# Attention in a macaron block: late features, turns and projections of group 5, and the placing of the first half moved to other steps

## The chip, the cores and the metric

One core of a Trainium2 chip runs the whole program. The metric is the device time of one execution in microseconds. The kernel before was timed in three runs; their median is 1233.25 us.

## What is computed

The reference takes x of 2 x 2048 tokens of 256 features and adds three blocks to it, each on a layer-normalized x: half of a mixture-of-experts feed-forward (16 experts in 4 groups of 4, top 2 of the best 2 groups, and a shared expert), an attention, and the same feed-forward again.

```python
x = x + 0.5 * ffn(layernorm(x), ...)
x = x + attn(layernorm(x), ...)
x = x + 0.5 * ffn(layernorm(x), ...)
```

The attention has 16 heads. Per head, the query and the key are each the normalized exterior product (6 numbers) of two projections to 4 numbers; scores are their product with a fixed signed permutation, times 6 to the power −0.5, causal, with a softmax over 2048 keys; values have 16 numbers per head; the result is projected by W_o and added to x.

## The kernel before

The program is one long sequence for each engine, ordered by semaphores. First comes the first feed-forward, then a stage called `lines`, then the attention (`attend`), then the second feed-forward by halves of the tokens (`ffn_by_halves`), whose routing for the first half of the tokens is done during the attention.

**`lines`** (L1258 to L1651) goes over 8 blocks of 512 tokens and makes from each the queries' and keys' features (fp16, split in a high and a low part) and the values. PE transposes the features ("turns", L1420), ScalarE evicts them from PSUM (L1496) and SP stores them to DRAM. The last block's features are done late, inside the first group of the attention: `copy_last` (two ScalarE copies, L1468 and L1469, after DVE's subtractions up to L1646), four `turn_last` parts on PE (L1449, two for queries and two for keys) and four `keep_last` evictions on ScalarE (L1461). SP stores queries and keys of that block after the second and the fourth eviction.

**`attend`** (L1686) goes over 8 groups g = 0 to 7: batch 0 has groups 0 to 3, batch 1 has groups 4 to 7 (`GATE` is 4), each with 4 heads. A group has four query chunks of 512 (`qc` 0 to 3) against key tiles of 128. The scores of the 40 units (one query chunk, one key tile, four heads) are packed in N = 48 strips of three PSUM banks, and each strip is one step i = 0 to 47:

- PE: `scores(g, i)` (L1877) into one of two strips of PSUM, then the value matmuls of the units that are due (`weigh`, L1903, four heads of 32 columns side by side), then what else is assigned to the step: a use of a spare bank, a late turn, a half projection (`project`, L1917).
- ScalarE: one exponential over the strip (L2017), from PSUM to a ring of 8 strips in SBUF. Scores of step i wait for the exponential of step i − 2.
- POOL: the causal masks (`cut`, L2027): ten selects for each chunk's diagonal, in its four strips (0 to 3, 8 to 11, 20 to 23 and 40 to 43): two, two, three and three.
- DVE: for each chunk, after its last values: copy of the sums (L2072), shuffle, reciprocal and product (L2075 to L2083), the "division"; then the additions of projections to x (`add_half`, L2097), statistics for the second normalization (L152) and pieces of routing.

Which values are due at which step is computed (L1727 to L1734). Values are due at steps 4, 6 to 9, 12, 14 to 17, 19 to 21, 24, 26 to 29, 31 to 33, 35 to 37, 39 to 41, 44 and 46 to 49 (48 and 49 are the next group's 0 and 1). Steps 6, 14, 26 and 46 have two narrow units (384 and 256 columns), steps 7, 15, 27 and 47 one of 128 and one of 512, the others one of 512. So steps 5, 10, 11, 13, 18, 22, 23, 25, 30, 34, 38, 42, 43 and 45 have no value matmuls ("free" steps). Chunk 0 and 2 sum in bank 6, chunk 1 and 3 in bank 7.

What else is done at a step is written by hand in tables (L1742 to L1763): the half projections of even groups at 22 and 25, of odd groups at 22, 25, 34, 38, 42 and 45; in group 5 ("shared") the last four are at 39, 41, 43 and 45. Projections use bank 7 for chunk 0 and 3 and bank 6 otherwise. In group 4 and 5 the normalized tokens of the first half are turned (`turn_at`, PE L1191) and copied by DVE (`keep_tiles`, L2110); the routing's logits are made at (5, 34) (PE L1959) and turned at (5, 38) (L1965); the pairs are counted at (6, 45) (PE L1196 and L1197). `rested` counts uses of the spare banks, so that each waits for the one before. DVE does the softmax, the choice and the weights in group 6, the placing (`routing.place`, L1109 to L1145) in group 7 after chunk 0, and `name_experts` after chunk 1. `add_among_marks` (L2165) holds the rest: the marks of rows (L1152), tiles (L1158) and tokens (L1163, L1167) among the additions of chunks 1 and 2 of group 7; PE's `invert` needs them after the attention.

An order by hand is one per engine: an instruction that waits holds all that stand behind it on its engine.

## Time and profile before

| | us |
|---|---|
| runs of the kernel before | 1233.25, 1230.09, 1234.88 (median 1233.25) |
| the profiled execution | 1235.22 |
| its span (first to last instruction) | 1233.5 |
| attention in it, first exponential to last values | 403.8 to 913.6 |
| PE busy | 1046.1 (85%) |
| ACT busy | 873.3 (71%) |
| DVE busy | 772.3 (63%) |
| POOL busy | 457.8 (37%) |

Times in the rows are microseconds from the span's start. PE is TensorE (matmuls), ACT ScalarE, DVE VectorE, POOL GpSimd, SP SyncE. A row of a timeline has the start, the length, the engine, the line of the kernel, the operation with its output and input, the shape and how many equal ones were merged; what stands in brackets is the idle time of the engine just before and what released it. A row of windows has the stretch and its length, then busy time and, in parentheses, instructions of PE, PE's weight loads, DVE, ACT and POOL, then TensorE's granted clock (1.00 is 2.4 GHz, 0.50 is 1.2 GHz), the DMA's busy share and GB/s.

### The profile page before, as it was taken

What the parts mean: (1) busy time and instruction counts of PE and PEld (TensorE: products, weight loads), DVE (VectorE), ACT (ScalarE), POOL (GpSimd) and SP (SyncE); (2) the same over time, 40 slices, a digit from 0 to 9 for tenths busy, and PEclk for the clock granted to TensorE, in tenths of its full rate; (3) what the DMA queues carried; (4) which work ended last, traced back from release to release, by engine and by line L of the source; (5) the groups of instructions that cost most, each with busy time, mean ns of one, the idle gap of its engine ahead of it and who ended that gap; (6) DMA issues with size and microseconds to landing.
All of it is one profiled execution on the core that took longest, in us unless ns stands there. A gap on an engine that the chain in (4) does not pass through costs nothing.

```text
span 1233.5 us, 23530 instructions
## 1 busy us (share of the span) xinstructions
PE 1046.1 (85%) x7487; PEld 570.4 (46%) x7487; DVE 772.3 (63%) x1565; ACT 873.3 (71%) x1250; POOL 457.8 (37%) x675
## 2 busy tenths in 40 slices
PE   3998999877887688988898989897999886967894
PEld 3457888744555212222222222221245685957752
DVE  6897777665997423444355565675786873645845
ACT  4246776624878999999999999999972463745610
POOL 1004555375630324331313234313133446564363
PEclk8999999998989799999999999999999997998997
DMA  8902544443756211010101130201009443443453
GB/s 294 279 4 78 161 152 156 130 127 108 219 176 213 88 31 52 18 52 18 52 18 53 35 104 19 74 15 52 2 31 318 127 137 124 155 137 114 131 167 120
DMA packets 125717, 133.79 MB, mean 108 GB/s; under 512 B 13224, under 2 KB 111888, under 8 KB 125616
## 3 DMA queue, kind: packets, MB, share of 16 engines
q1 hardware_dynamic: 109056, 90.95, 23.2%
q0 software_dynamic: 14448, 39.47, 11.1%
q10 hardware_dynamic: 2112, 2.10, 0.5%
q8 instruction: 55, 0.90, 0.3%
q14 instruction: 46, 0.38, 0.1%
HBM read 80.43 MB, written 52.04 MB: 107 GB/s over the span
## 4 chain that ended last, share of the span: by engine, by line
PE 30%; ACT 23%; issue 14%; DVE 7%; another core or an unknown queue 4%; DVEq 1%; ACTq 0%
ACT wide L2017 19%; PE banks L1903 6%; PE banks L2391 5%; PE banks L2316 3%; PE banks L2403 2%; PE banks L1877 2%; PE banks L2325 2%; PE banks L1433 2%; PE banks L1436 1%; PE banks L2379 1%; PE banks L1362 1%; DVEq L2599 1%; PE banks L1420 1%; PE banks L1917 1%
## 5 line engine op out<-in xcount | busy, mean ns | idle before, releaser
L2017 ACT ACTIVATE wide<-banks 128x1536 f32<-128x1536 f32 (+1 forms) x384 | 492.6, 1475 | 9.9 <-PE banks L1877 8.5
L1903 PE MATMUL banks<-wide,attn_attend_v_now 128*32 128x512 f32 (+3 forms) x2560 | 290.9, 546 | 1.9 <-ACT wide L2017 1.0
L2027 POOL TENSOR_SCALAR_AFFINE_SELECT wide<-wide 128x256 f32<-128x256 f32 (+1 forms) x320 | 115.3, 389 | 398.9 <-ACT wide L2017 396.4
L1877 PE MATMUL banks<-attn_attend_q_now,attn_attend_k_now 32*128 32x512 f16 (+3 forms) x1280 | 151.6, 357 | 55.6 <-ACT wide L2017 52.6
L1877 PEld LDWEIGHTS banks<-attn_attend_q_now,attn_attend_k_now 32*128 32x128 f16 x1280 | 38.8, 91 | 292.7 <-ACT wide L2017 243.2
L2391 PE MATMUL banks<-f_xnt 128*128 128x128 f32 x752 | 108.3, 290 | 39.0 <-ACT f_xnt L2476 19.2
L651 POOL DMA_INDIRECT f_region<-xn_rows,f_token_of x79 | 77.3, 978 | 137.1 <-DVE f_token_of L882 84.8
L2391 PEld LDWEIGHTS banks<-f_xnt 128*128 128x128 f32 x752 | 97.3, 202 | 46.5 <-ACT f_xnt L2469 25.3
L2072 DVE COPY sums<-banks 128x512 f32<-128x512 f32 x32 | 22.1, 692 | 141.9 <-PE banks L1903 141.6
L2077 DVE RECIPROCAL below<-below 128x512 f32<-128x512 f32 x32 | 107.3, 3353 | 1.1
L2499 POOL DMA_INDIRECT last_rows_in<-xn_rows,f_spare x72 | 69.6, 967 | 78.1 <-DVE f_stage L2560 24.5
L520 PE MATMUL banks<-f_region,wide 128*128 128x128 f32 x632 | 86.5, 280 | 6.4 <-issue 3.4
L1903 PEld LDWEIGHTS banks<-wide,attn_attend_v_now 128*32 128x32 f32 x2560 | 57.0, 109 | 75.1 <-issue 72.7
L520 PEld LDWEIGHTS banks<-f_region,wide 128*128 128x128 f32 x632 | 78.0, 194 | 10.1 <-issue 6.7
L2469 ACT ACTIVATE f_xnt<-last_w_all 128x514 f32 x94 | 59.4, 632 | 30.2 <-issue 23.7
L2483 ACT ACTIVATE f_xnt<-banks,f_xnt 128x128 f32<-128x128 f32 x94 | 34.3, 364 | 55.4 <-PE banks L2391 37.6
L1341 POOL DMA_INDIRECT f_region<-y_slots,attn_lines_rows_of x64 | 64.0, 1000 | 23.6 <-issue 17.1
L2610 DVE TENSOR_TENSOR f_xnt<-banks,last_w_down 128x256 f32<-128x256 f32 x94 | 39.4, 419 | 47.7 <-PE banks L2403 27.9
L619 ACT ACTIVATE wide<-f_w_all 128x514 f32 x79 | 49.9, 632 | 26.7 <-issue 23.6
L2403 PE MATMUL banks<-last_w_down,f_more 128*128 128x256 f32 x188 | 59.1, 397 | 1.0 <-DVE f_more L2617 1.0
L2097 DVE TENSOR_TENSOR x_res<-banks,x_res 128x512 f32<-128x512 f32 x30 | 20.7, 690 | 61.9 <-PE banks L1917 61.8
L2602 DVE COPY last_w_down<-last_w_all 128x512 f32 x94 | 41.5, 441 | 27.3 <-issue 23.8
(365 smaller groups left out, 1799.6 us busy)
## 6 DMA issues: line engine op xcount, KB each, us to landing
y_half<-f_xnt SPq DMA_DIRECT2D x94, 128.0 KB
y_slots<-wide SPq DMA_DIRECT2D x79, 128.0 KB
attn_v<-f_more SPq DMA_DIRECT2D x32, 256.0 KB
attn_attend_v_now<-attn_v SPq DMA_DIRECT2D x32, 256.0 KB, 3.3
x_res<-L_attn_x SPq DMA_DIRECT2D x8, 512.0 KB, 7.6
xn_rows<-f_w_all SPq DMA_DIRECT2D x8, 512.0 KB, 4.5
attn_q<-attn_lines_q_out SPq DMA_DIRECT2D x8, 512.0 KB
attn_k<-attn_lines_k_out SPq DMA_DIRECT2D x8, 512.0 KB
```

The source lines that it names most:

```text
L520: last = pe.matmul(bank[2 + m][:, f * P:(f + 1) * P], w_up[:, at, col_at:col_at + INTER], rows_t[:, m, c * P:(c + 1) * P], start=(c == 0), ...
L651: pool.indirect_dma_start(out=rows_in[:, n % ROUND, :], out_offset=None, in_=xn_rows, in_offset=bass.IndirectOffsetOnAxis(ap=token_of[:, n ...
L1341: pool.indirect_dma_start(out=back[:, q, j, k, :], out_offset=None, in_=y_slots, in_offset=bass.IndirectOffsetOnAxis(ap=rows_of[:, q, j, k ...
L1877: last = pe.matmul(score[i % SLOTS][:, j, column:column + columns(u)], k_now[rows, kt * P:(kt + 1) * P], q_now[rows, qc * QW + c0:(qc + 1) ...
L1903: last = pe.matmul(out_bank[qc][rows, c0:QW], v_now[:, kt, rows], probs[:, place, column:column + columns(u)], start=(kt == 0), stop=(u == ...
L2017: act.activation(probs_flat[:, at:at + width_of[i]], score_flat[i % SLOTS][:, 0:width_of[i]], ACT.Exp, scale=SCALE).then_inc(sem.exp_done, 1)
L2027: pool.affine_select(out=part, in_=part, compare_op=ALU.is_ge, fill=0.0, base=0, pattern=[[0, part.shape[1]], [1, P]], channel_multiplier= ...
L2077: dve.reciprocal(below[:], below[:]).then_inc(sem.chain_step, 1)
L2391: last = pe.matmul(bank[2 + m][:, f * P:(f + 1) * P], w_up[:, at, col_at:col_at + INTER], rows_t[:, m, c * P:(c + 1) * P], start=(c == 0), ...
L2403: pe.matmul(bank[4 + m][:, 0:D], prod_t[:, at, :], w_down[:, at, 0:D], start=True, stop=True).then_inc(sem.y_done, 1)
L2469: act.activation(w_up[:, n % ROUND, :], w_all[:, bass.ds(expert, 1), 0:UP].rearrange("p o f -> p (o f)"), ACT.Copy).then_inc(sem.up_kept, 1)
L2499: pool.indirect_dma_start(out=rows_in(n), out_offset=None, in_=xn_rows, in_offset=bass.IndirectOffsetOnAxis(ap=s.token_of[:, place_of_turn ...
```

## The change

It moves work to other steps and changes what waits for what; no instruction is added or left out.

- Late features in group 0: the copies follow exponential 4 instead of 1; turns and evictions are at steps 18, 20, 22 and 25 instead of 3, 5, 9/10 and 11/12, all in bank 7. The values of chunks 1 and 2 no longer wait for the features, those of chunk 3 do; the first turn waits for chunk 1's sums, the third for the second eviction.
- Group 5: the last two turns of tokens at 21 and 23 instead of 18 and 20; half projections at 25, 28, 38, 41, 43, 45 instead of 22, 25, 39, 41, 43, 45; the logits' turn at 36 instead of 38.
- Group 6: the count at 42 instead of 45, then the placing and the naming of experts behind it on DVE, which stood in group 7.
- Group 7: the first half of chunk 2's projection is added to x before the marks of tokens instead of after them.

```diff
--- before.py
+++ after.py
@@ -1658,7 +1658,7 @@
 HALF_HEADS = (2, 0, 3, 1)
 
 
-PROJECT_7, PROJECT_6, PROJECT_6_LATE = (22, 25), (34, 38, 42, 45), (39, 41, 43, 45)
+PROJECT_7, PROJECT_6, PROJECT_LATE = (22, 25), (34, 38, 42, 45), (25, 28, 38, 41, 43, 45)
 
 
 def units_and_banks():
@@ -1741,7 +1741,7 @@
 
     two_of_0, four_of_1 = ((0, 0), (0, 1)), ((1, 0), (1, 1), (2, 0), (2, 1))
     project_at = {0: dict(zip(PROJECT_7, ((QC - 1, 0), (QC - 1, 1)))), 1: dict(zip(PROJECT_7 + PROJECT_6, two_of_0 + four_of_1)),
-                  "shared": dict(zip(PROJECT_7 + PROJECT_6_LATE, two_of_0 + four_of_1))}
+                  "shared": dict(zip(PROJECT_LATE, two_of_0 + four_of_1))}
     proj_bank = lambda qc, half: banks[:, 7 if qc in (0, QC - 1) else 6, :]
 
     def projected_before(two, qc, half):
@@ -1751,16 +1751,15 @@
     GATE = GROUPS
     projections = lambda g, side: project_at["shared" if g == GATE + 1 else side]
     turn_at = {(GATE, 38): (0, 0), (GATE, 42): (0, 1), (GATE, 45): (1, 0), (GATE, 47): (1, 1),
-               (GATE + 1, 10): (2, 0), (GATE + 1, 13): (2, 1), (GATE + 1, 18): (3, 0), (GATE + 1, 20): (3, 1)}
-    weights_at, logits_at, logits_turn_at, count_at, exp_at = (GATE, 34), (GATE + 1, 34), (GATE + 1, 38), (GATE + 2, 45), (GATE + 2, 4)
-    assert max(i for g, i in (logits_at, logits_turn_at)) < min(PROJECT_6_LATE) and turn_at.keys().isdisjoint({(GATE + 1, i) for i in range(PROJECT_7[0], 33)})
+               (GATE + 1, 10): (2, 0), (GATE + 1, 13): (2, 1), (GATE + 1, 21): (3, 0), (GATE + 1, 23): (3, 1)}
+    weights_at, logits_at, logits_turn_at, count_at, exp_at = (GATE, 34), (GATE + 1, 34), (GATE + 1, 36), (GATE + 2, 42), (GATE + 2, 4)
+    assert max(i for g, i in (logits_at, logits_turn_at)) < PROJECT_LATE[2] and turn_at.keys().isdisjoint({(GATE + 1, i) for i in range(PROJECT_LATE[0], 33)})
     rest_uses = sorted([*turn_at, weights_at, logits_at, logits_turn_at, count_at])
 
-    late_at = {(0, 3): 0, (0, 5): 1, (0, 9): 2, (0, 11): 3}
-    late_bank = lambda part: banks[:, 7 - part // 2, :]
-    kept_at = {(0, 3): 0, (0, 5): 1, (0, 10): 2, (0, 12): 3}
-    copied_at = (0, 1)
-    assert pv_step[last_of[0]] < 9 and pv_step[last_of[0] + 1] > 5 and pv_step[last_of[1] + 1] > 11
+    late_at = {(0, 18): 0, (0, 20): 1, (0, 22): 2, (0, 25): 3}
+    late_bank = banks[:, 7, :]
+    copied_at = (0, 4)
+    assert pv_step[last_of[1]] < 18 and pv_step[last_of[2] + 1] > 25
 
     def rested(g, i):
 
@@ -1888,8 +1887,8 @@
                 pe.wait_ge(sem.masked, MASKS * g + masks_of[u])
             if kt == 0 and (later(g) or qc > 1):
                 pe.wait_ge(sem.sums_kept, QC * g + qc - 1)
-            if kt == 0 and g == 0 and qc in (1, 2):
-                pe.wait_ge((lines_sem.q_ready, lines_sem.k_ready)[qc - 1], 2 * BLOCKS)
+            if kt == 0 and g == 0 and qc == QC - 1:
+                pe.wait_ge(lines_sem.k_ready, 2 * BLOCKS)
             if kt == 0 and qc == QC - 1:
                 if side == 1:
                     pe.wait_ge(sem.proj_added, projected_before(two, 0, 1) + 1)
@@ -1929,9 +1928,11 @@
                 use_rest(g, i)
             if (g, i) in late_at:
                 part = late_at[g, i]
-                if part == 2:
-                    pe.wait_ge(sem.sums_kept, 1)
-                rest.turn_last(pe, part, late_bank(part))
+                if part == 0:
+                    pe.wait_ge(sem.sums_kept, 2)
+                elif part == 2:
+                    pe.wait_ge(lines_sem.q_ready, 2 * BLOCKS)
+                rest.turn_last(pe, part, late_bank)
             if i in projections(g, side) and (later(g) or side == 1):
                 qc, half = projections(g, side)[i]
                 copied = QC * g + (QC - 2 if qc in (0, QC - 1) else QC - 1)
@@ -2018,8 +2019,8 @@
                                ).then_inc(sem.exp_done, 1)
                 if (g, i) == copied_at:
                     rest.copy_last(act)
-                if (g, i) in kept_at:
-                    rest.keep_last(act, kept_at[g, i], late_bank(kept_at[g, i]))
+                if (g, i) in late_at:
+                    rest.keep_last(act, late_at[g, i], late_bank)
 
         groups(group)
 
@@ -2151,9 +2152,7 @@
                 routing.weigh(dve, 0)
                 routing.keep_counts(dve, 0, rest_bank(count_at[1]))
                 dve.sem_inc(sem.rest_kept, 1)
-            elif g == GATE + 3 and qc == 0:
                 routing.place(dve, 0)
-            elif g == GATE + 3 and qc == 1:
                 routing.name_experts(dve, 0)
 
         def sum_block(two, qc):
@@ -2170,8 +2169,8 @@
             routing.mark_tiles(dve)
             add_half(two, 1, 1)
             sum_block(two, 1)
+            add_half(two, 2, 0)
             routing.mark_tokens(dve)
-            add_half(two, 2, 0)
             add_half(two, 2, 1)
             sum_block(two, 2)
 
```

## Rows read from the trace of the kernel before

**Rows 1.** Windows: groups 0, 2, 5; length, busy us (instructions) per engine, granted clock, DMA.

```profile
403.80:474.10 70.30, 56.11 (x497) 14.62 (x501) 20.21 (x24) 66.91 (x55) 23.11 (x44) 0.87 0.14 44
...
535.50:596.60 61.10, 52.44 (x492) 13.12 (x489) 24.45 (x23) 61.01 (x50) 13.68 (x40) 1.00 0.12 36
...
719.70:785.20 65.50, 60.68 (x544) 18.43 (x540) 38.54 (x53) 62.09 (x48) 24.09 (x45) 1.00 0.16 50
```

**Rows 2.** Timeline of ACT, group 0: start, length; idle before in brackets.

```profile
407.21 0.84 ACT L1468 ACTIVATE f_xnt<-f_xnt 128x768 f16<-128x768 f16 x1 [1.03 <-DVE f_xnt L1646]
...
420.93 1.24 ACT L2017 ACTIVATE wide<-banks 128x1280 f32<-128x1280 f32 x1 [0.45 <-PE banks L1877]
...
422.07 1.02 ACT L1461 ACTIVATE attn_lines_k_out<-banks 128x1024 f16<-128x1024 f16 x1
...
445.37 26.33 ACT L2017 ACTIVATE wide<-banks 128x1536 f32<-128x1536 f32 x20 [0.85 <-PE banks L1877]
...
472.44 1.45 ACT L2017 ACTIVATE wide<-banks 128x1536 f32<-128x1536 f32 x1 [0.73 <-PE banks L1877]
```

**Rows 3.** Timeline of PE, group 0, at both clocks.

```profile
410.60 1.94 PE L1903 MATMUL banks<-wide,attn_attend_v_now 128*32 128x512 f32 x8
...
417.62 1.06 PE L1903 MATMUL banks<-wide,attn_attend_v_now 128*32 128x512 f32 x8
...
419.93 0.62 PE L1449 MATMUL banks<-ident,f_xnt 128*128 128x128 f16 x8
```

**Rows 4.** Windows: stretches at the lower granted clock.

```profile
401.00:414.60 13.60, 7.32 (x53) 2.44 (x51) 5.70 (x12) 11.53 (x13) 3.83 (x10) 0.50 0.35 116
...
441.95:445.36 3.41, 3.41 (x26) 0.84 (x30) 0.00 (x0) 2.58 (x2) 3.41 (x2) 0.50 0.00 0
...
865.20:868.61 3.41, 3.41 (x31) 0.71 (x22) 3.12 (x9) 1.88 (x2) 0.00 (x0) 0.50 0.02 5
```

**Rows 5.** Timelines of DVE, PE and ACT, group 5.

```profile
745.96 0.68 DVE L2110 COPY f_xnt<-banks 128x512 f32<-128x512 f32 x1
...
746.75 0.63 PE L1191 MATMUL banks<-ident,f_stage 128*128 128x128 f32 x4 [1.09 <-issue]
...
747.75 2.56 ACT L2017 ACTIVATE wide<-banks 128x1280 f32<-128x1280 f32 x2 [1.29 <-PE banks L1877]
...
775.90 1.13 PE L1917 MATMUL banks<-attend_w_o,heads 128*128 128x256 f32 x4
...
777.41 10.37 ACT L2017 ACTIVATE wide<-banks 128x1280 f32<-128x1280 f32 x8 [1.15 <-PE banks L1877]
```

**Rows 6.** Timeline of POOL: masks of groups 5, 6 and 7.

```profile
733.62 2.89 POOL L2027 TENSOR_SCALAR_AFFINE_SELECT wide<-wide 128x256 f32<-128x256 f32 x6 [0.51 <-ACT wide L2017]
...
840.79 2.14 POOL L2027 TENSOR_SCALAR_AFFINE_SELECT wide<-wide 128x256 f32<-128x256 f32 x6 [0.48 <-ACT wide L2017]
...
860.63 3.64 POOL L2027 TENSOR_SCALAR_AFFINE_SELECT wide<-wide 128x256 f32<-128x256 f32 x6 [0.51 <-ACT wide L2017]
...
904.23 3.83 POOL L2027 TENSOR_SCALAR_AFFINE_SELECT wide<-wide 128x256 f32<-128x256 f32 x6 [0.48 <-ACT wide L2017]
```

**Rows 7.** Timelines of PE and ACT, groups 6 and 7.

```profile
843.48 1.28 PE L1903 MATMUL banks<-wide,attn_attend_v_now 128*32 128x384 f32 x16
...
866.65 1.45 ACT L2017 ACTIVATE wide<-banks 128x1536 f32<-128x1536 f32 x1 [1.02 <-PE banks L1877]
...
869.19 4.14 ACT L2017 ACTIVATE wide<-banks 128x1536 f32<-128x1536 f32 x3 [1.09 <-PE banks L1877]
...
907.69 1.10 PE L1917 MATMUL banks<-attend_w_o,heads 128*128 128x256 f32 x4 [1.86 <-DVE x_res L2097]
...
909.16 2.99 ACT L2017 ACTIVATE wide<-banks 128x1536 f32<-128x1536 f32 x2 [1.28 <-PE banks L1877]
```

**Rows 8.** Timeline of DVE, group 7: first and last of the placing's 19 instructions.

```profile
861.96 0.41 DVE L1118 TENSOR_REDUCE f_spare<-f_region 128x16 f32<-128x256 f32 x1
...
868.94 0.18 DVE L1145 SCALAR_TENSOR_TENSOR f_spare<-f_spare 128x32 bf16<-128x32 f32 x1
```

## The prediction, made before the changed kernel was run

> **What bounds the kernel now.** I read the windows of the eight groups first. ScalarE is busy for 61.0 of group 2's 61.1 us: the exponentials, one per step, set the pace, about 1.33 us for a full step and 1.12 for a narrow one. Group 0 takes 70.3 us and group 5 takes 65.5 [rows 1]. So the change can gain only what ScalarE idles in groups 0, 5, 6 and 7, and the timeline of ACT names every such gap with its releaser; the timelines of PE, DVE and POOL say why the releaser was late. Consecutive exponentials overlap by some 0.15 us in these rows (twenty in 26.33, though one lasts 1.45 [rows 2]), so a gap costs its idle time and about 0.15 more. TensorE is nearly as full: a step with one key tile is 0.32 us of scores and 1.0 of value matmuls [rows 3] against 1.33, so it can be pushed over the edge by small things. At the lower of its two clock levels (1.2 instead of 2.4 GHz) the same eight matmuls take 1.94 instead of 1.06 us [rows 3].
>
> **Part 1, late features (group 0).** The work stays: two copies of 0.84 and four evictions of 1.02 us on ScalarE [rows 2], four turns of 0.62 on TensorE [rows 3]. What goes is waiting.
> (a) ScalarE stood 1.03 us before the copies, for DVE's last subtraction [rows 2]. At step 4 DVE has long ended: −1.0.
> (b) The eviction at step 10 follows a step that waited 0.45 for PE [rows 2], because PE ran at 1.2 GHz for the first 13.6 us [rows 4] and had turns between. Without turns there it has less to do in a shorter time. If the clock rises as before, steps 7 to 9 still wait: 0 to 1.2 us in place of 0.6. I take 0.4: −0.2.
> (c) At step 26 ScalarE waited 0.85 [rows 2], as PE's clock fell for 3.4 us [rows 4] after steps in which it had little to do. The turns at 18, 20, 22 and 25 put work there, and the eviction after step 25 lengthens ScalarE's side by 0.9, so a slower PE would be covered. Bounds 0 and −1.4; I take −1.2, the nearer to the row with what follows it.
> A rule speaks against (c). The Trainium skill's page "TensorE: Matmul & The Clock Gate", section "Part 4: PE-mode transpose", says that transposes do not count as busy for the clock. By it the turns would not hold the clock and the sum would be 1.2 smaller; no row here isolates that.
> (d) Step 46 lost 0.73 and a little more in the same way [rows 2]. Nothing is changed there, group 2 shows no such gap [rows 1], and shifted in time any even group may: 0, bounds −1.3 and +1.3.
> SP's stores of the last block's features come later (after steps 20 and 25), with the loads of group 1 behind them; those are used from step 48 on, and the last block is read first in group 4: 0. If that cover were gone, group 1 would start late, which no gap now hints at. The waits before value blocks 1 and 2 go, and one before block 3 (step 31) comes, five steps after its release: 0. The turns at 18 and 22 wait for a sum already kept and for the eviction of step 20. The latter holds PE about 1 us in a step without value matmuls: 0.
>
> **Part 2, group 5.** Before, the turn at step 20 waited for DVE, which copied the one of step 18 only at 745.96, after its division; PE started at 746.75 and ScalarE idled 1.29 [rows 5]. With two narrow steps behind it that ran at PE's pace (1.32 instead of 1.12 us) this is 1.85. At steps 21 and 23 DVE is free. A turn of 0.63 beside one key tile at step 21 makes PE late by 0.2: −1.65 in all.
> The projection moved from step 22 (no value matmuls) to 28 is the cost. Steps 26 and 27 have 1.28 us of value matmuls each, as at 843.48 [rows 7], to which 0.3 of scores come. With a projection at 25 as before, PE needs 1.45, 1.55 and 1.55 us in three steps of 1.33 and is 0.55 late at 28. Some 0.8 can be made up (1.33 less the scores' 0.4 and a little), so another 1.13 of projection there stalls ScalarE for 0.9. The nearest row agrees: step 41 has a projection beside a key tile too, and ScalarE idled 1.15 after it [rows 5]. Bounds 0.4 and 1.3; I take +0.9. DVE's addition of it moves too; the next division, queued behind, needs step 29 anyway. For value block 3 at step 31 PE now waits for an addition that ends about two steps earlier: 0.
> Of the rest, the projection at 39 goes to 38, a free step (about −0.7), but the logits' turn goes from free 38 to 36, beside a key tile, when PE is still late from the logits (+0.6); the stall at 41 stays. Zero together. Part 2: −0.75.
>
> **Part 3, placing.** In group 7 the placing's 19 DVE instructions (861.96 to 869.12 [rows 8]) ran beside POOL's masks of steps 10 and 11. These six selects took 3.64 us, against 2.89 in group 5, which has the same division beside them but no placing [rows 6]. The masks were 0.75 late, PE waited, its clock fell at 865.2 [rows 4], and ScalarE idled 1.02 and 1.09 [rows 7]. Removed: −2.4 (of it 0.6 by the masks alone, the rest by the clock).
> It now runs at the end of group 6, after a count that is three steps earlier: the selects at 840.79 follow exponential 42 [rows 6], and the count, behind the scores of its step, ends some 1.4 us ahead of them, at 839.4. So the placing runs from about 840.2 to 847.4 and the naming of the experts to 848.5. PE's last values of the group start at 843.48 [rows 7] and need two double steps of 1.5 and two of 1.3 us: DVE's next division starts near 849, so that is free. But the last six selects of that group run from 840.79 for 2.14 us [rows 6], and PE needs them at 843.48 [rows 7]: 0.55 us of room. Stretched by the same 0.75 they end at 843.7, and with the scan and two additions all in their way at 844.4. PE may be about 0.4 late before it shows on ScalarE. Bounds 0 and 1.0 (more if the clock falls too); I take +0.4.
> This trace shows selects longer beside DVE's operations, not which rule decides. The Trainium skill's page "SBUF — State Buffer", section "SBUF: two separate sides", says that a DVE operation with two SBUF inputs holds the shared port for its whole length. By it this term would be 1.0; the observed 0.75 is between.
> Last, in group 7 the first half of projection 2 is added before the token marks. The next projection waited 1.86 for that addition and ScalarE 1.28 [rows 7]. That wait ends, but the masks (3.83 us from 904.23, to 908.06 [rows 6]) are slowed by the same marks, which now run 0.7 later, and end near 908.3: PE starts the next values there instead of at 909.05. Bounds 0 and −1.5; −0.7.
>
> **Sum:** −1.0 −0.2 −1.2 −0.75 +0.4 −2.4 −0.7 = −5.85. The profiled execution took 1235.22 us (span 1233.5), so 1229.4. It is 2.0 above the median, 1233.25. Of the 5.85, about 3.0 are stalls by a fallen clock (1.2 and 1.8), which another execution may not have had; with half of them the median gives 1233.25 − 4.35 = 1228.9. I say **1229.0**. What follows the attention is a chain of its own that starts earlier and takes its time.
>
> **The rivals.**
> Better: the projection at 28 costs 0.4, the placing in group 6 nothing, and the gap at 46 goes with the shift: −0.5 −0.4 −1.3, so 1226.8. For it: each is a bound from a row; against it: the lateness at 28 was worked out from steady rows.
> The clock falls in spite of the turns, at step 26: +1.2, 1230.2. For it: ScalarE's evictions stretch these steps, so PE has less to do per time than before. Against it: the eviction after 25 covers part.
> The placing only moves its damage: late masks in group 6, in steps with neither projection nor count, then the fallen clock as in group 7. Price 2.1 more, 1231.1.
> It does not do what it says: parts 2 and 3 cancel within themselves (projection at 28 for the turn, group 6 for group 7, the marks still in the way): only part 1 is left, 1232.8.
> Slower: the clock falls between the spread turns of steps 22 to 25 and stays low as long as at the group's start, 13.6 us [rows 4]. A full step then costs 0.55 + 1.9 = 2.45 us instead of 1.33, so 5.5 steps lose 6, and (c) is lost: 1229.0 + 1.2 + 6 = 1236.2. It decides from the third such step on. For it: PE waits on ScalarE there. Against it: both later falls in this trace ended after 3.4 us.
>
> **How the numbers follow.** Forecast 0.36 (its own range 1226.5 to 1231.5), better 0.24, clock at 26 0.15, placing 0.13, not what it says 0.07, slower 0.05. A measurement of this kernel can tell about 0.5%, 6.2 us, from no change: under 1227.1 is faster. That is nearly all of better (0.22) and a fifth of the forecast (0.08): 0.30. Slower by over 0.5% (1239.4) needs eight low steps, more than half of that rival: 0.03. The rest, 0.67, is the same. The range reaches from the forecast less both bounds at 46 and 28, and a little, 1224.5, to the case where only part 1 works, 1233.
>
> **What the profile after would show.** Group 0 takes 67.5 to 68.5 us, with no gap before the copies and the granted clock high at step 26; group 5 about 64.7, with a gap of some 0.9 after step 28 and none after 20; in group 6 the last six selects take 2.9 us or more, with at most a small gap at step 47; in group 7 the six selects of steps 10 and 11 take 2.9, no gap follows step 14, and the gap at 46 is about half. The prediction is wrong if the clock falls at other steps for more than 3.4 us, if group 5 does not get shorter, or if group 6 gets longer by over 1.5 us.

## The result and the profile after

| | before | after |
|---|---|---|
| median of the runs timed together, 12 each (us) | 1234.07 | 1228.24 |
| ratio, with its 95% interval | | 0.9951 (0.9929 to 0.9973) |
| profiled execution (us) | 1235.22 | 1224.65 |
| its span | 1233.5 | 1222.7 |
| attention, first exponential to last values | 509.8 | 502.8 |
| from there to the end, code unchanged | 319.9 | 314.9 |

The change makes the kernel 5.8 us faster; 1229.0 had been predicted. The two profiled executions differ by 10.6 us, more than the medians: the one after lies 3.6 under its median, the one before 1.2 above. Only 7.0 of the 10.6 are in the attention, which began 1.2 us later. The 5.0 behind it belong to code that nobody touched; what moved them was not looked into, and two later profiles of the changed kernel took 323.1 and 325.7 us there. So the attention's 7.0 us are the figure to set against the sum of the prediction, 5.85.

ScalarE paces the attention, so its waits come first. Of the kernel before, in the attention alone (engine, what waited for what, us in total, times, longest):

```profile
ACT wide L2017 <- PE banks L1877: 8.5, 10, 1.3
...
ACT f_xnt L1468 <- DVE f_xnt L1646: 1.0, 1, 1.0
```

and of the kernel after:

```profile
ACT wide L2018 <- PE banks L1876: 3.5, 5, 1.2
```

The eleven waits have become five, and 9.5 us have become 3.5. The instructions are the same in number, and busy time hardly moved, as the line of the profile's page after shows:

```profile
PE 1043.9 (85%) x7487; PEld 568.9 (47%) x7487; DVE 771.7 (63%) x1565; ACT 872.7 (71%) x1250; POOL 457.7 (37%) x675
```

Windows of groups 0, 2, 5 and 7 after (columns as in [rows 1]):

```profile
405.00:471.90 66.90, 56.41 (x497) 14.27 (x501) 20.20 (x24) 66.31 (x54) 23.54 (x44) 0.88 0.14 45
...
533.20:594.30 61.10, 52.45 (x492) 13.12 (x491) 24.44 (x23) 61.01 (x49) 13.69 (x40) 1.00 0.12 36
...
717.40:782.30 64.90, 60.88 (x544) 18.48 (x540) 38.45 (x53) 62.05 (x49) 24.10 (x45) 1.00 0.16 50
...
843.90:906.40 62.50, 56.46 (x509) 16.05 (x508) 45.93 (x79) 61.61 (x49) 19.09 (x43) 1.00 0.06 16
```

Group 0 went from 70.3 to 66.9 us and group 5 from 65.5 to 64.9. Group 2, where nothing changed, took 61.1 in both. Group 7, counted from its first exponential to its last, went from 64.0 to 61.0; the window shown reaches to the end of its last exponential. Group 6 is 0.2 longer.

**Group 0.** Timeline of ACT after (start, length; idle before in brackets):

```profile
404.99 5.97 ACT L2018 ACTIVATE wide<-banks 128x1280 f32<-128x1280 f32 x5
...
410.80 0.88 ACT L1468 ACTIVATE f_xnt<-f_xnt 128x768 f16<-128x768 f16 x1
...
412.26 18.39 ACT L2018 ACTIVATE wide<-banks 128x1536 f32<-128x1536 f32 x14
...
430.44 1.12 ACT L1461 ACTIVATE attn_lines_q_out<-banks 128x1024 f16<-128x1024 f16 x1
...
441.61 1.26 ACT L1461 ACTIVATE attn_lines_k_out<-banks 128x1024 f16<-128x1024 f16 x1
...
442.51 3.25 ACT L2018 ACTIVATE wide<-banks 128x1536 f32<-128x1536 f32 x2
...
446.17 28.38 ACT L2018 ACTIVATE wide<-banks 128x1536 f32<-128x1536 f32 x22 [0.40 <-PE banks L1876]
```

Nothing stands in the copies' brackets: they follow five exponentials at once, where ScalarE had stood 1.03 us [rows 2]. The fourteen exponentials behind them run through, so the wait of the old step 10 is gone too. A gap near step 26 is still there, 0.40 in place of 0.85 us. It now stands one step later, and the step before it was some 0.5 late as well. Its cause is in the windows of low clock and in PE's timeline:

```profile
441.37 2.36 PE L1902 MATMUL banks<-wide,attn_attend_v_now 128*32 128x384 f32 x16
...
403.90:414.10 10.20, 6.69 (x43) 1.32 (x43) 4.55 (x11) 10.19 (x10) 3.83 (x10) 0.50 0.28 97
...
438.10:444.90 6.80, 6.60 (x53) 2.27 (x49) 0.00 (x0) 6.70 (x7) 5.76 (x7) 0.50 0.15 52
```

The clock after 438.1 was 0.50 for 6.8 us, through steps 23 to 27, although the turns stood there. The double value matmuls of step 26 took 2.36 instead of 1.28 us. Before, the fall lasted 3.4 us [rows 4]. The other low stretch, from the attention's start, ended at 414.1, 10.2 us after it began; before, it lasted 13.6 [rows 4].

**Group 5.** Timelines of PE and ACT:

```profile
752.84 1.06 PE L1902 MATMUL banks<-wide,attn_attend_v_now 128*32 128x512 f32 x8
...
753.84 1.13 PE L1916 MATMUL banks<-attend_w_o,heads 128*128 128x256 f32 x4
...
754.90 0.39 PE L1876 MATMUL banks<-attn_attend_q_now,attn_attend_k_now 32*128 32x512 f16 x3
...
755.34 10.95 ACT L2018 ACTIVATE wide<-banks 128x1536 f32<-128x1536 f32 x8 [0.81 <-PE banks L1876]
...
766.72 6.58 ACT L2018 ACTIVATE wide<-banks 128x1536 f32<-128x1536 f32 x5 [0.43 <-PE banks L1876]
...
774.44 11.70 ACT L2018 ACTIVATE wide<-banks 128x1280 f32<-128x1280 f32 x9 [1.15 <-PE banks L1876]
```

The gap of 1.29 after step 20 [rows 5] has gone. The projection at step 28 brings one of 0.81: it follows the value matmuls on PE, the next scores start only behind it, at 754.90, and the exponential waits for them. The waits at 36 and 41 are 0.43 and 1.15.

**Groups 6 and 7.** Timeline of POOL, the six selects of the end of group 6, of steps 10 and 11 and of the end of group 7:

```profile
837.82 2.75 POOL L2028 TENSOR_SCALAR_AFFINE_SELECT wide<-wide 128x256 f32<-128x256 f32 x6 [0.48 <-ACT wide L2018]
...
857.88 2.89 POOL L2028 TENSOR_SCALAR_AFFINE_SELECT wide<-wide 128x256 f32<-128x256 f32 x6 [0.51 <-ACT wide L2018]
...
899.16 3.95 POOL L2028 TENSOR_SCALAR_AFFINE_SELECT wide<-wide 128x256 f32<-128x256 f32 x6 [0.48 <-ACT wide L2018]
```

Those of steps 10 and 11 take 2.89 in place of 3.64 [rows 6]; those of group 6 stretch from 2.14 to 2.75, where the placing now is. Timelines of DVE and PE there: the placing's scan, the last instruction of the naming, and the value matmuls that need the masks.

```profile
837.83 0.94 DVE L1119 TENSOR_TENSOR_SCAN f_region<-ones,f_region 128x256 f32<-128x256 bf16 x1
...
845.37 0.18 DVE L1179 CAST slots<-f_spare 128x32 int32<-128x32 f32 x1
...
840.72 1.28 PE L1902 MATMUL banks<-wide,attn_attend_v_now 128*32 128x384 f32 x16
```

The masks end at 840.57 and the matmuls start at 840.72: 0.2 later than the 843.48 of [rows 7] less the 2.97 us by which the selects start earlier. The naming ends at 845.5, and DVE's next division starts at 846.2. In group 7 the timeline of ACT has one gap left, of 0.76, where there were three [rows 7]:

```profile
854.13 50.02 ACT L2018 ACTIVATE wide<-banks 128x1280 f32<-128x1280 f32 x39
...
904.91 1.45 ACT L2018 ACTIVATE wide<-banks 128x1536 f32<-128x1536 f32 x1 [0.76 <-PE banks L1876]
```

### The profile page after: what moved, and what is told of

Same layout as the page of the kernel before. It is cut to its first block, busy times and chain, and to the rows that moved or that the text cites. A ratio compares the mean times of both kernels' runs of the same rounds, so it can differ in the third digit from the quotient of the medians.

```text
span 1222.7 us, 23529 instructions
## 1 busy us (share of the span) xinstructions
PE 1043.9 (85%) x7487; PEld 568.9 (47%) x7487; DVE 771.7 (63%) x1565; ACT 872.7 (71%) x1250; POOL 457.7 (37%) x675
## 4 chain that ended last, share of the span: by engine, by line
PE 30%; ACT 24%; issue 15%; DVE 6%; another core or an unknown queue 3%; DVEq 1%; POOL 0%; ACTq 0%; POOLq 0%
ACT wide L2018 21%; PE banks L2390 6%; PE banks L1902 5%; PE banks L2315 4%; PE banks L2402 3%; PE banks L1876 2%; PE banks L2324 2%; PE banks L1433 2%; PE banks L1436 2%; PE banks L2378 1%; PE banks L1362 1%; PE banks L1435 1%; PE banks L1420 1%; DVEq L2598 1%
## 5 line engine op out<-in xcount | busy, mean ns | idle before, releaser
L1341 POOL DMA_INDIRECT f_region<-y_slots,attn_lines_rows_of x64 | 64.3, 1005 | 23.6 <-issue 17.1
L2098 DVE TENSOR_TENSOR x_res<-banks,x_res 128x512 f32<-128x512 f32 x30 | 20.7, 690 | 65.8 <-PE banks L1916 65.7
```

The costliest lines, as they stand in the source:

```text
L1341: pool.indirect_dma_start(out=back[:, q, j, k, :], out_offset=None, in_=y_slots, in_offset=bass.IndirectOffsetOnAxis(ap=rows_of[:, q, j, k ...
```

## The experiments

Each kernel was timed in a series with the kernel before on one chip, and times are compared by ratio within a series, as the chips differ (below). The ratio is not that of the two medians and can differ from it: in `part1_late` the medians alone give 0.9980. "Late by" means how much longer the distance from an exponential to the next was than for the same step in the steady groups 1 to 4, read from the exponentials of each trace. Each kernel is told by its difference from the kernel before, except where another is named.

**The three parts alone.** `part1_late` has the hunks of the diff on the late features alone, with the waits at the value blocks and before the turns.

```diff
-    late_at = {(0, 3): 0, (0, 5): 1, (0, 9): 2, (0, 11): 3}
-    late_bank = lambda part: banks[:, 7 - part // 2, :]
-    kept_at = {(0, 3): 0, (0, 5): 1, (0, 10): 2, (0, 12): 3}
-    copied_at = (0, 1)
...
+    late_at = {(0, 18): 0, (0, 20): 1, (0, 22): 2, (0, 25): 3}
+    late_bank = banks[:, 7, :]
+    copied_at = (0, 4)
...
```

> Only the late features are moved. Theory A (gaps by name): group 0 loses the 1.03 us before the copies and most of the 0.6 near step 10; it takes 67 us if the granted clock falls once near step 26 and 66 if not, against 70.3 before, and groups 1 to 7 stay as they were (65.6 in group 5, 64.0 in group 7). In the time: 2.5 to 4 us less. Rival B (the gain of the whole change is mostly the placing, and group 0 was only lucky in its clock): under 1.5 us less.

Measured: 0.9968 (0.9953 to 0.9982), 1159.34 against 1161.71 us. Group 0 took 65.8 us, nothing was lost at step 26. Windows at low clock, of group 0 and of group 7, and ACT's timeline of group 7:

```profile
411.60:415.00 3.40, 3.40 (x21) 1.00 (x19) 0.00 (x0) 3.40 (x4) 2.36 (x7) 0.51 0.03 9
...
834.90:841.70 6.80, 5.96 (x41) 1.59 (x41) 5.64 (x19) 4.11 (x3) 1.30 (x3) 0.50 0.01 2
...
839.29 1.45 ACT L2018 ACTIVATE wide<-banks 128x1536 f32<-128x1536 f32 x1 [1.74 <-PE banks L1876]
...
842.02 38.70 ACT L2018 ACTIVATE wide<-banks 128x1536 f32<-128x1536 f32 x30 [1.27 <-PE banks L1876]
...
882.00 2.99 ACT L2018 ACTIVATE wide<-banks 128x1536 f32<-128x1536 f32 x2 [1.28 <-PE banks L1876]
```

In group 0 the clock fell here as well, for 3.4 us over steps 22 to 25, and no exponential came late. In group 7, where this kernel still has the placing, the clock fell behind the late masks and cost 3.3 us in two gaps.

`part2_g5` has group 5's tables alone.

```diff
-PROJECT_7, PROJECT_6, PROJECT_6_LATE = (22, 25), (34, 38, 42, 45), (39, 41, 43, 45)
+PROJECT_7, PROJECT_6, PROJECT_LATE = (22, 25), (34, 38, 42, 45), (25, 28, 38, 41, 43, 45)
...
-                  "shared": dict(zip(PROJECT_7 + PROJECT_6_LATE, two_of_0 + four_of_1))}
+                  "shared": dict(zip(PROJECT_LATE, two_of_0 + four_of_1))}
...
-               (GATE + 1, 10): (2, 0), (GATE + 1, 13): (2, 1), (GATE + 1, 18): (3, 0), (GATE + 1, 20): (3, 1)}
-    weights_at, logits_at, logits_turn_at, count_at, exp_at = (GATE, 34), (GATE + 1, 34), (GATE + 1, 38), (GATE + 2, 45), (GATE + 2, 4)
...
+               (GATE + 1, 10): (2, 0), (GATE + 1, 13): (2, 1), (GATE + 1, 21): (3, 0), (GATE + 1, 23): (3, 1)}
+    weights_at, logits_at, logits_turn_at, count_at, exp_at = (GATE, 34), (GATE + 1, 34), (GATE + 1, 36), (GATE + 2, 45), (GATE + 2, 4)
...
```

> Only group 5's turns, projections and logits' turn are moved. Theory A: the stall of 1.45 us after step 20 and the two short ones behind it go, 1.0 us comes after step 28 and 0.55 after step 36 for the 0.58 after 39, so group 5 takes 64.9 us for 65.6: 0.7 us less, within the noise of the time. Rival B (the stall at 28 is there only because of what group 0 shifted): no stall after step 28 and 63.9 us.

Measured: 0.9984 (0.997 to 0.9998). Group 5 took the 64.9 us expected. Steps were late by 0.33 at 21, 0.98 at 28, 0.55 at 36 and 1.27 at 41, to 0.02 us as in the whole change.

`part3_placing` has the count at 42, the placing and naming in group 6, and the marks of tokens behind the first addition of chunk 2.

```diff
-    weights_at, logits_at, logits_turn_at, count_at, exp_at = (GATE, 34), (GATE + 1, 34), (GATE + 1, 38), (GATE + 2, 45), (GATE + 2, 4)
+    weights_at, logits_at, logits_turn_at, count_at, exp_at = (GATE, 34), (GATE + 1, 34), (GATE + 1, 38), (GATE + 2, 42), (GATE + 2, 4)
...
-            elif g == GATE + 3 and qc == 0:
                 routing.place(dve, 0)
-            elif g == GATE + 3 and qc == 1:
                 routing.name_experts(dve, 0)
...
+            add_half(two, 2, 0)
             routing.mark_tokens(dve)
-            add_half(two, 2, 0)
```

> Only the count, the placing, the naming and the order of the marks in group 7 are moved. Theory A: group 7 loses the gaps after steps 14 and 15 (2.4 us) and half of the one after 45 (0.5 to 0.7), group 6 gains 0.2: 2.8 us less, of which 1.8 only where the clock had fallen at step 14 of group 7 before. Rival B (the clock's fall at step 14 is chance and not the placing's): without it before, the gain is 1.2 us or less.

Measured: 0.9968 (0.9955 to 0.998). Group 7 took 61.0 us, late by 0.98 at step 46 and nowhere else; its six selects took 2.89, those of group 6 2.75 us. Group 6 took 63.1, but 1.3 of that stand at steps 6 to 8 behind a fall of the clock in a stretch that no part touches.

The three ratios add to −0.80%; the whole change measured −0.49% at first, and −0.54 and −0.97% in later series. With an uncertainty of 0.12 to 0.36% on each, that neither shows nor excludes that something is lost between the parts. The groups' lengths tell more: each part changes its own groups as it does in the whole.

**Part 3 split.** `placing_only` has the first two hunks of the diff above, `marks_only` has the last.

> Only the count, the placing and the naming are moved to group 6; the marks stay ahead of the addition. Theory A: the last six selects of group 6 take 2.75 us for 2.14 and cost ScalarE 0.2 after step 47; group 7 loses the gaps after 14 and 15 (2.3 to 3.2 us here) and keeps the one of 1.48 after 45: 2 to 3 us less than before. Rival B (the clock's fall at step 14 of group 7 is chance): with the six selects back at 2.9 us a gap of over 1 us stays there.

Measured: 0.999 (0.9964 to 1.0017), 1242.43 us. No gap follows steps 14 and 15 of group 7. But the end of group 7 was worse than before, as ACT shows:

```profile
912.32 1.45 ACT L2017 ACTIVATE wide<-banks 128x1536 f32<-128x1536 f32 x1 [1.77 <-PE banks L1877]
...
914.94 1.45 ACT L2017 ACTIVATE wide<-banks 128x1536 f32<-128x1536 f32 x1 [1.16 <-PE banks L1877]
```

These are 1.77 and 1.16 in place of 1.28 [rows 7]: the clock fell at 911.1 for 3.4 us, just after PE had waited 1.9 us for the addition behind the marks. The 2 to 3 us less that were expected are not shown by the time, and group 7 became only 0.75 us shorter. That the clock falls at this place looks like chance: the marks stand ahead of the addition in three other kernels (before and the two parts without its move) and it did not fall there.

> Only the order of the marks and the first addition of chunk 2 in group 7 is changed. Theory A: the 1.48 and 0.21 us after steps 45 and 46 become one gap of 0.97 after 46, since POOL's six selects still take 3.9 us beside the marks: 0.7 us less, and the gaps after 14 and 15 stay. Rival B (the addition was all that PE waited for): no gap after 45 or 46, 1.7 us less.

Measured: 0.9986 (0.9955 to 1.0016), 1241.33 us. Window of the low clock and ACT's timeline of group 7:

```profile
866.40:869.80 3.40, 3.26 (x28) 1.19 (x32) 3.13 (x9) 1.66 (x3) 0.00 (x0) 0.50 0.02 5
...
869.49 1.45 ACT L2017 ACTIVATE wide<-banks 128x1536 f32<-128x1536 f32 x1 [1.74 <-PE banks L1877]
...
871.22 40.04 ACT L2017 ACTIVATE wide<-banks 128x1536 f32<-128x1536 f32 x31 [0.29 <-PE banks L1877]
...
912.03 1.45 ACT L2017 ACTIVATE wide<-banks 128x1536 f32<-128x1536 f32 x1 [0.76 <-PE banks L1877]
```

The last gap is 0.76, as in the whole change, from the marks' move alone, and the masks of steps 10 and 11 are late and the clock falls behind them, as before. In the profiles of this study ScalarE waited after step 14 of group 7, with the clock low, in all four kernels with the placing there (before, the two parts without its move, this one), and in none of the ten others did it lose time there. Four in four against none in ten: so it is the placing beside the masks that brings this fall, not chance. The times of both halves fit no gain as well as one of 4 us; here only the traces tell.

**Does the work of turns hold the clock?** `turns_four_times` is the changed kernel with each late turn made four times over. It leaves nothing out and adds redundant work.

```diff
-        for g in (2 * pair, 2 * pair + 1):
-            for j in range(BT):
+        for again in range(4):
+            for g in (2 * pair, 2 * pair + 1):
+                for j in range(BT):
```

> The changed kernel with the eight fp16 transposes of each late turn made four times over, into the same places: at steps 18, 20, 22 and 25 of group 0 PE is occupied for about 2.4 us instead of 0.6. Theory A (transposes do not hold the clock): the granted clock falls between steps 19 and 27 of group 0, as turns fill the free steps, and group 0 takes 2 us or more above the changed kernel's 66.0 to 66.9. Rival B (they count like other work of PE): it stays at 1.00 there and ScalarE loses only what PE is late, about 1 us at each turn beyond the eviction's shadow.

PE and the window over steps 18 to 27:

```profile
437.24 1.96 PE L1450 MATMUL banks<-ident,f_xnt 128*128 128x128 f16 x32
...
433.00:450.00 17.00, 16.23 (x221) 9.20 (x218) 2.63 (x2) 15.62 (x15) 7.17 (x12) 1.00 0.12 41
```

A turn made four times took 1.96 us instead of 0.62 (2.4 had been expected), and the clock stayed high all through group 0 once it had risen. Of the 16.2 busy us in this window 7.5 are turns. ScalarE waited for PE as PE was now full, 1.04 us at the most, and group 0 took 68.0 us; the time, 1240.33 in one run, says nothing at this size.

`plain_beside_turns` puts 24 plain matmuls of the same size before each turn instead, again redundant.

```diff
+        for again in range(24):
+            pe.matmul(into[:, again % 4 * P:again % 4 * P + P], core.ident16[:],
...
```

> The changed kernel with 24 plain fp16 matmuls of the transposes' shape (128x128 by 128) ahead of each late turn, overwritten by it: PE is occupied for about as long as with the turns made four times. Theory A: these count, so the clock stays at 1.00 from step 18 to 28 of group 0. Rival B (nothing at these steps holds the clock): it falls there as in the changed kernel's first profile (from 438.1 for 6.8 us).

```profile
436.00:453.00 17.00, 16.23 (x222) 9.47 (x223) 2.90 (x2) 15.27 (x14) 6.89 (x12) 1.00 0.10 35
```

The clock stayed high here as well, with PE just as busy. (Group 0 took 69.1 us; of these, 1.3 stand behind a fall at steps 13 and 14, ahead of the turns.) So transposes and plain matmuls could not be told apart: nothing showed transposes to count for less. It is one profile each, and of the seven profiles with the late features at 18 to 25 and no extra work, two had no fall there either.

**A version that may be better.** `best_both` is the changed kernel with group 5's last turns at 18 and 21, its first projections at 23 and 25 (so none beside the double steps' backlog), and the marks after both additions of chunk 2.

```diff
-PROJECT_7, PROJECT_6, PROJECT_LATE = (22, 25), (34, 38, 42, 45), (25, 28, 38, 41, 43, 45)
+PROJECT_7, PROJECT_6, PROJECT_LATE = (22, 25), (34, 38, 42, 45), (23, 25, 38, 41, 43, 45)
...
-               (GATE + 1, 10): (2, 0), (GATE + 1, 13): (2, 1), (GATE + 1, 21): (3, 0), (GATE + 1, 23): (3, 1)}
+               (GATE + 1, 10): (2, 0), (GATE + 1, 13): (2, 1), (GATE + 1, 18): (3, 0), (GATE + 1, 21): (3, 1)}
...
+            add_half(two, 2, 1)
             routing.mark_tokens(dve)
-            add_half(two, 2, 1)
```

> The changed kernel with three more edits: in group 5 the last two turns at steps 18 and 21 and the first two half projections at 23 and 25, in group 7 the marks of tokens after both additions of chunk 2. Theory A: the 0.98 us after step 28 of group 5 goes (projection in a free step; the turn at 18 is copied at about 746, before 21), and the 0.97 us after step 46 of group 7 goes, since the masks no longer stand beside the marks: 1.9 us less than the changed kernel, about 7.5 less than before, group 5 63.9 us and group 7 60.0. Rival B (the projection at 28 is only one of two causes, lateness from the double steps 26 and 27 is enough): a stall of 0.5 us or more stays after step 26 to 29.

Measured: 0.9928 (0.9915 to 0.9942), 1154.32 us. Timelines of ACT (group 5), POOL, DVE (the marks) and PE (end of group 7):

```profile
721.61 19.97 ACT L2018 ACTIVATE wide<-banks 128x1280 f32<-128x1280 f32 x15 [0.36 <-PE banks L1876]
...
874.45 2.14 POOL L2028 TENSOR_SCALAR_AFFINE_SELECT wide<-wide 128x256 f32<-128x256 f32 x6 [0.47 <-ACT wide L2018]
...
877.83 1.75 DVE L1163 TENSOR_TENSOR f_region<-f_region,tile_of_pair 128x1536 bf16<-128x1536 bf16 x1
...
877.37 1.28 PE L1902 MATMUL banks<-wide,attn_attend_v_now 128*32 128x384 f32 x16
```

Group 5 took 64.2 us: the stall at 28 is gone, and step 21, late by 0.53, is all that came for it. Group 7 took 60.0: with no marks beside them the six selects took 2.14 instead of 3.95, and no gap is left.

`changed_again` is the changed kernel once more. `best_steps` is `best_both` with these steps:

```diff
-PROJECT_7, PROJECT_6, PROJECT_LATE = (22, 25), (34, 38, 42, 45), (23, 25, 38, 41, 43, 45)
+PROJECT_7, PROJECT_6, PROJECT_LATE = (22, 25), (34, 38, 42, 45), (23, 25, 38, 42, 43, 45)
...
-               (GATE + 1, 10): (2, 0), (GATE + 1, 13): (2, 1), (GATE + 1, 18): (3, 0), (GATE + 1, 21): (3, 1)}
+               (GATE + 1, 10): (2, 0), (GATE + 1, 13): (2, 1), (GATE + 1, 18): (3, 0), (GATE + 1, 22): (3, 1)}
```

> The changed kernel itself, on the chip of the other runs. Theory A (the three parts add): about 8 us less than before, the sum of the three single parts (2.4, 1.8 and 2.8 us), and groups 5, 6 and 7 as in its first profile (64.9, 61.7, 61.0 us). Rival B (they take from one another, and the 6.0 us of the first comparison is the whole): 5.5 to 6.5 us less.

> As the version with three more edits, with two steps of group 5 changed again: the last turn at 22 instead of 21 and the second half of the projection of chunk 1 at 42 instead of 41, both free steps. Theory A: the stall of 0.53 us after step 21 goes, the 1.27 and 0.17 us at 41 and 40 go, and 0.6 us comes near step 43 or 44, since the next half projection waits for DVE's addition of this one: group 5 takes 63.1 to 63.4 us against 64.2. Rival B (the addition holds PE longer than that): a stall of over 1.2 us after step 43, and no gain.

Measured: 0.9946 (0.9922 to 0.997), about 6.7 us less than before, and 0.9952 (0.9926 to 0.9979). `changed_again` had the lengths of the groups again (64.9, 61.7 and 61.0 for the last three); in group 0 the clock fell for 3.4 us and cost nothing. `best_steps` missed what was expected of group 5: 64.9 instead of 63.1 to 63.4. ACT's timeline of it:

```profile
757.51 18.07 ACT L2018 ACTIVATE wide<-banks 128x1536 f32<-128x1536 f32 x13 [0.33 <-PE banks L1876]
...
786.10 10.79 ACT L2018 ACTIVATE wide<-banks 128x1536 f32<-128x1536 f32 x8 [0.80 <-PE banks L1876]
```

The wait of 1.15 at 41 went, but one of 0.80 came at 43, where the projection follows that of 42: late by 0.91. At 23 to 27 the later turn cost another 0.9, against 0.5 at step 21.

Last, best and changed kernel side by side, `best_again` and `changed_third`:

> The version with three more edits (turns at 18 and 21, half projections at 23 and 25, marks after both additions), again, beside the changed kernel on one chip. Theory A: group 5 takes 64.2 and group 7 60.0 us as before, 1.6 us less together than the changed kernel, 7 to 9 us less than the kernel before. Rival B (the difference was that chip's): no difference from the changed kernel.

> The changed kernel, beside the version above. Theory A: about 6 us less than before (0.9946 to 0.9951 of it so far), 1.6 us more than the version above. Rival B: equal to it.

Measured: 0.9912 (0.9883 to 0.9941), 1236.82 us, and 0.9903 (0.9867 to 0.9938), 1235.62 us. The groups repeated: 64.25 against 64.90 and 60.05 against 60.99, 1.6 us between them. The times don't resolve 1.6 us (0.13%) and leave open whether this version is faster; that it waits less in groups 5 and 7 stands in both of its profiles.

## Why the prediction was right, and where it was not

The time and the sign were right: 1228.2 measured, 1229.0 said. The gain between the medians was sized a little low, 4.25 from 1233.25, where 5.8 from 1234.07 were measured: the forecast had halved the 3.0 us of clock stalls as things that might be absent, and the largest of them, in group 7, turned out to be there in every kernel with the placing beside the masks. Term by term, by how late each step was in the two profiles (after less before):

| step of the prediction | said | measured |
|---|---|---|
| (a) wait before the copies | −1.0 | −1.2 |
| (b) steps 7 to 10 | −0.2 | −0.35 |
| (c) clock at step 26 | −1.2 | −0.4 |
| (d) step 46 | 0 | −1.4, by chance |
| part 2, group 5 | −0.75 | −0.67 |
| part 3, placing out of group 7 | −2.4 | −2.4 |
| part 3, placing into group 6 | +0.4 | +0.2 |
| part 3, marks | −0.7 | −0.7 |
| sum | −5.85 | −6.9 |

In (a) the idle time that went is the 1.03 said; steps 1 to 4 together took 1.16 less, as such a gap costs its idle time and some 0.15 more. The last 0.1 to 7.0 is in small differences. That the sum comes so near is luck in part: −1.4 of it is the chance of step 46, where no other kernel with the early features lost anything, and it covers what (c) fell short. Since one profile has chance falls of the clock in it, the lengths of all profiles are the better test of part 1: group 0 took 67.5 to 70.3 us in the five kernels with the early features (mean 68.6) and 65.8 to 67.0 in the seven with the late ones and no extra work (mean 66.4). That is −2.2 for part 1, where −2.4 was said, and with −0.7, −3.1 and +0.2 for the others it comes to −5.8, as much as between the medians. Of (b), part may be the clock at the attention's start: step 9 was late by 0.20 in the two kernels with early features whose low stretch there lasted 10.2 us, and by 0.48 to 0.56 in the three where it lasted 13.6; it was 10.2 in the profile after, where step 8 was late by 0.18.

**Right, and shown.** (a): no idle time stands before the copies any more. The zero for SP's later stores holds: group 1 took 61.2 to 61.4 us in all seven profiles with the late features and no extra work, as with the early ones. Part 2: the projection at 28 costs what was worked out (0.98 late; +0.9 said), it is there in `part2_g5` and gone in `best_both`. The turn at 21 cost 0.33 for 0.2. The zero for steps 34 to 41 is −0.15: 36 costs 0.55 (+0.6 said), 39 gives 0.58 (−0.7 said), the rest is at 34 and 40. Part 3: the selects fell to 2.89 as said, and the clock's fall behind them went with the lateness, the chain of 0.6 and 1.8 that had been put at −2.4. The marks: 1.69 became 0.97, in `marks_only` too.

**Wrong: step (c).** "The turns at 18, 20, 22 and 25 put work there" was to hold the clock. They did not: the clock fell between steps 22 and 25 in five of the seven profiles with the late features there, about as often as with the early ones, three of five. What seems to save the time is the second half of that step, the eviction after step 25: with the late features, where the fall lasted 3.4 us (three of the five) it cost nothing. In `part2_g5`, without evictions there, a fall of 3.4 us over the same steps, 23 to 25, cost 0.92. That ScalarE's 0.9 for the eviction gave PE the time to catch up is the reading of these rows, not tried by itself. Where it lasted 6.8 us (the profile after, `best_both`) it cost 1.0. Over the profiles the stretch lost 0.7 us on average with the early features (0.92, 1.37 and 1.38 in three of five) and 0.3 with the late ones (0.99 twice in seven), so as a mean this term is some −0.4 rather than −1.2. The rival "clock at 26" (0.15) came true in the profile, at +0.8 instead of +1.2, and (d), which happened to go the other way by 1.4, hid it in this one profile. The rule set against (c), that transposes do not count for the clock (the Trainium skill, "TensorE: Matmul & The Clock Gate", "Part 4: PE-mode transpose"), would have made the term 0, nearer to the −0.4 than what was said, but the runs don't bear out its reason, as far as one profile tells: with four times the turns the clock stayed at 1.00, though the 7.5 us of turns left only 8.7 of the 17 us to other work. The prediction's own sign of being wrong, a fall at other steps for more than 3.4 us, was met in the profile after, by this fall of 6.8 us over steps 23 to 27, and group 0's 66.9 us lie below the 67.5 to 68.5 that it named only by the chance of step 46.

**Sized too high: placing in group 6.** The selects were put at 2.89, they took 2.75, and PE was 0.2 late instead of 0.4. The rule that a DVE operation with two SBUF inputs holds the shared port for its whole length (the Trainium skill, "SBUF — State Buffer", "SBUF: two separate sides") was to give 1.0, from the scan and two additions added up. Read select by select the trace agrees with the rule, and it is the adding up that fails. Timelines of DVE and POOL after, at the marks, each in a window that holds this one instruction:

```profile
899.84 1.75 DVE L1163 TENSOR_TENSOR f_region<-f_region,tile_of_pair 128x1536 bf16<-128x1536 bf16 x1
...
899.90 1.84 POOL L2028 TENSOR_SCALAR_AFFINE_SELECT wide<-wide 128x128 f32<-128x128 f32 x1
```

This select takes 0.29 us alone; here it started 0.06 behind the mark and ended 0.15 after it. Beside the placing the selects behind the scan and behind the two additions ended 0.20, 0.16 and 0.26 after them, and so were 0.38, 0.18 and 0.20 longer than alone: each waits only for what is left of the DVE operation when it starts, and then ends sooner than its own length after it. In all, the six became 0.61 longer. The scan took 0.94 here and 0.69 at 959.07, with no select near; it started 0.01 behind a select of 0.41, so here it was DVE that came second. Rival "placing only moves its damage" is refuted by this and by `part3_placing`.

**The chances.** Slower is excluded by the interval, "not what it says" by the parts. The ratio's 0.49% lies on the border of the half per cent between "the same" (0.67) and "faster" (0.30); later series gave 0.54 and 0.97%. The range's lower end, 1224.5, does not follow from its working: 1229.0 less 1.3 and 0.5 is 1227.2, and even "better" was put at 1226.8.

## What to carry to other kernels

Where one engine paces a loop, an edit to the order of another is worth the gaps it closes less those it opens: list them per step, in the steady groups and in the odd ones, and cost each by the work that its releaser has in the two steps ahead. A projection of 1.1 us cost 0.9 to 1.3 where PE was already behind (28, 41, 43 here) and nothing where the steps before had left it free (23, 25, 38). A mask late by 0.7 us can cost 2.4, when the engine that waits for it loses its clock, so move what slows the mask first; and read (and time) such a kernel more than once, as clock falls in sparse stretches come and go by themselves at 1 us each.

## What the runs showed of the hardware

- **Selects on POOL wait for some DVE operations and not for others.** In the profiles before and after, the selects that started while DVE ran a scan, addition or product of 0.4 us or more with both inputs in SBUF ended 0.15 to 0.27 us after it, whatever they took alone (up to 0.39 where one started at the very end of the operation). A bf16 operation of 0.62 us with one input, the last of the marks, held one back as well. The 74 selects beside the reciprocals of 3.35 us (one input) and the 13 or 14 beside additions that read PSUM kept their 0.29 or 0.41. So six selects of 2.14 us took 2.43 or 2.89 beside a division, 2.75 beside the placing, 3.64 beside both, and 3.83 to 3.96 beside marks of 128x1536 bf16. It goes the other way too: the mark of 1.75 us took 1.97 before, where it started 0.08 behind a select.
- **The clock falls in steady stretches too**, in places that differ from one execution to the next: steps 43 to 45 of group 2 (1.1 us lost, `part1_late` and `best_both`), 4 to 6 of group 6 (1.3, `part3_placing` and `placing_only`), 11 to 15 of group 0 (0 to 1.3, five kernels). Steps without value matmuls are in or just before each of these places. The falls windowed here lasted 3.4 or 6.8 us; the stretch from the attention's start is longer, 10.2 to 17.1.
- **Chips differ outside the attention.** The kernel before took 1161.7 us on the chip of the three parts and of `best_both`, and 1234 to 1246 in the other series. The attention took as long there: 501.8 us in `best_both` against 500.2 in `best_again`, 506.9 in `part3_placing` against 507.9 in `placing_only`. It began at 380 instead of 404 to 414 us, and what stands behind it took 270 instead of 315 to 327. Which transfers or instructions are slower there was not looked into.
